# LoRA product from f16 halves with powers of two, in 512-column chunks and PSUM banks of its own, and another order of y's transposes

## The reference, cut to what matters

```python
x = x + tanh(g_xattn) * matmul(fake_quant(layernorm(x)), fake_quant(ctx))    # x: 2 x 1024 x 2048
y = layernorm(x)
logits = y @ gate_w.T + expert_bias                                          # 4 experts
one_hot = onehot(argmax(logits))
base = y @ W_up.T                                                            # 2048 x 2048
z = einsum('nh,erh->ner', y, lora_A)                                         # rank 8 for each expert
delta = einsum('neh,ne->nh', einsum('ner,ehr->neh', z, lora_B), one_hot)
x = x + tanh(g_ffn) * (base + delta)
```

## Time and profile before

| | us |
|---|---|
| median of 3 runs | 967.28 (966.79 to 969.95) |
| the profiled execution, its own time | 968.11 |
| its span, first to last instruction | 966.3 |
| TensorE busy | 938.9 |
| VectorE busy | 411.3 |
| ScalarE busy | 229.9 |
| products of stage 2 (line 980), 3840 matmuls | 686.7 |
| products of stage 1 (line 912), 1024 matmuls | 226.4 |
| `lora` (line 987), 80 matmuls | 29.1 |

### The profile page before, as it was taken

The page is one execution under the profiler, slowest core; times in us unless marked ns, Lnnn a source line. Parts: engine busy times, 40 slices in busy tenths (PEclk is TensorE's granted clock), DMA queues, the critical chain, the costliest instruction groups (busy, mean ns, idle before and its releaser), DMA issues.

```text
span 966.3 us, 12221 instructions
## 1 busy us (share of the span) xinstructions
PE 938.9 (97%) x5280; PEld 505.9 (52%) x5280; DVE 411.3 (43%) x829; ACT 229.9 (24%) x192; POOL 15.3 (2%) x39
## 2 busy tenths in 40 slices
PE   2899999999999999999999999999999999999998
PEld 0444444444455555555555555555555555555554
DVE  6694757785867404132332404232332404232301
ACT  5886777777540000000000000000000000000000
POOL 0001000000000000000000000000000000000000
PEclk9999999999999999999999999999999999999999
DMA  8999977678543233222322132222223222121211
GB/s 348 420 375 390 419 290 287 220 296 303 195 177 78 88 87 88 88 44 87 44 87 70 67 110 60 88 44 87 44 88 77 64 78 44 44 44 44 44 45 44
DMA packets 77018, 135.25 MB, mean 140 GB/s; under 512 B 61889, under 2 KB 62017, under 8 KB 62657
## 3 DMA queue, kind: packets, MB, share of 16 engines
q1 hardware_dynamic: 71200, 93.52, 29.7%
q0 software_dynamic: 3312, 24.12, 6.4%
q10 hardware_dynamic: 2448, 16.78, 4.2%
HBM read 90.36 MB, written 29.37 MB: 124 GB/s over the span
## 4 chain that ended last, share of the span: by engine, by line
PE 91%; DVE 4%; DMA 2%; ACT 1%; issue 1%; SPq 0%; DVEq 0%; ACTq 0%
PE bank L980 66%; PE bank L912 21%; PE bank L987 2%; PE bank L889 1%; DVE arena L660 1%; DMA stage<-in_b_t 1%; DMA rows<-in_x 1%; DVE bn L570 1%; DMA normed<-in_w 1%; ACT arena L396 1%; ACT arena L414 0%; DVE rows_T L680 0%; DVE rows L630 0%; DVE b_stack L721 0%; DVE halves L668 0%
## 5 line engine op out<-in xcount | busy, mean ns | idle before, releaser
L980 PE MATMUL bank<-arena,rows_T 128*128 128x416 f16 (+1 forms) x3840 | 686.7, 339 | 0.0
L980 PEld LDWEIGHTS bank<-arena,rows_T 128*128 128x128 f16 x3840 | 369.7, 97 | 302.8 <-issue 8.2
L912 PE MATMUL bank<-arena,rows_T 128*128 128x512 bf16 x1024 | 226.4, 382 | 3.2 <-ACT rows_T L388 2.3
L912 PEld LDWEIGHTS bank<-arena,rows_T 128*128 128x128 bf16 x1024 | 99.7, 98 | 122.2 <-issue 3.8
L728 DVE SCALAR_TENSOR_TENSOR rows<-bank,derived,rows 128x416 f32<-128x416 f32 (+2 forms) x80 | 48.4, 640 | 252.9 <-PE bank L987 252.9
L435 ACT ACTIVATE z_stack_T<-bank 96x128 fp32r<-96x128 f32 x16 | 4.4, 273 | 565.3 <-PE bank L994 565.3
L570 DVE BATCH_NORM_STATS2 bn<-rows 128x6 f32<-128x512 f32 x124 | 76.8, 680 | 6.0 <-DMA rows<-in_x 3.8
L630 DVE SCALAR_TENSOR_TENSOR rows<-bank,derived,rows 128x512 f32<-128x512 f32 x60 | 44.7, 747 | 23.8 <-PE bank L912 23.3
L694 DVE SCALAR_TENSOR_TENSOR route<-bank,derived,scal 128x4 f32<-128x4 f32 x16 | 3.5, 221 | 115.9 <-PE bank L980 115.8
L396 ACT ACTIVATE arena<-arena,scal,derived 128x2048 int16<-128x2048 f32 x22 | 45.0, 2084 | 2.8 <-DMA arena<-in_ctx 2.8
L670 DVE SCALAR_TENSOR_TENSOR halves<-normed,ln,halves 128x2048 f16<-128x2048 f32 x14 | 32.9, 2351 | 29.0 <-ACT halves L429 29.0
(11 more groups left out here) (89 smaller groups left out, 253.9 us busy)
## 6 DMA issues: line engine op xcount, KB each, us to landing
arena<-in_ctx SPq DMA_DIRECT2D x22, 1024.0 KB, 17.0
stage<-in_w SPq DMA_DIRECT2D x17, 1042.0 KB, 5.5
out<-rows ACTq DMA_DIRECT2D x15, 1024.0 KB, 3.9
h_scratch<-rows POOLq DMA_DIRECT2D x11, 1024.0 KB, 7.4
rows<-h_scratch SPq DMA_DIRECT2D x11, 1024.0 KB, 4.9
stage<-in_ctx SPq DMA_DIRECT2D x10, 1024.0 KB, 12.3
rows<-in_x POOLq DMA_DIRECT2D x10, 1024.0 KB, 9.4
normed<-in_w SPq DMA_DIRECT2D x7, 1042.0 KB, 6.3
```

Source lines behind the costliest of these rows:

```text
L912: mm = mmul(bk, q1T[:, t % 4, kt, :], Q(b, n, kt), start=(kt == 0), stop=(kt == KT - 1 and not slow), skip_group_check=True)
L980: mm = mmul(bank[c][:, 0:b - a], YT[:, s % 2, yh, kt, :], W(kt, wh, a, b), start=(first and kt == kts[0] and yh == 0 and wh == 0), stop=False,
```

## The change

- The stack of z and the B stack are f16 instead of f32 or fp32r. Ahead of that z (already multiplied with the scale of the product) is multiplied with a row of powers of two, one for each row of B, and divided by a power of two of its own token; B's rows are divided by theirs. `route` grows from 9 linked instructions to 14, and one more writes the factor that takes the scale back (`gl`).
- `lora` works in four chunks of 512 columns that go to banks 5 and 6 in turn, no more into the banks of the products. The last product of a chunk closes its group. Chunks 0 and 1 of `lora` stand behind chunk 2 of the products, chunks 2 and 3 behind chunk 3, and none behind chunk 4. For tile 0 they stand inside tile 1: chunks 0 and 1 behind its chunk 0, and 2 and 3 in the midst of its chunk 1.
- `epi2` waits for the products alone; a new `epi_delta` adds the LoRA part, four times for each tile. `store2` waits for both. On VectorE epi2(s, 0) stands ahead of the moments of the next tile.
- lora_B is loaded by POOL, ahead of the maximum over the partitions, into the row buffer 0. ScalarE sums its magnitudes after y_high(0), `b_scale` makes the powers in four small instructions after epi(15, 3), and POOL sends them through HBM to all partitions. ScalarE makes the high half after the last weight, and `b_low` makes the low one in place of `b_stack`. POOL's load of row tile 20 stands behind all that.
- Group (0, 2) of y's transposes goes to bank 7 and stands directly behind (0, 1). Tile 0 starts block by block as the groups come out. Groups (1, 2) and (1, 3) stand behind chunk 4 of tile 0, and their `yT_out` behind the `epi2` of tile 0. Tile 1 does blocks 0 to 7 of its chunks 0 and 1 ahead of the wait for the other groups.
- The f32 identity is gone.

```diff
...
-        with nc.sbuf_tensor("stage1", [P, WC], F32) as S1:
-            pass
-        Bst = sb("b_stack", [P, WC], F32R)[0:ZR, 0:D]
-        Braw = S1[0:ZR, 0:D]
+        S1 = sb("stage1", [P, WC], F32)
+        Bst = S1[:, :].bitcast(F16)[0:ZR, 0:D]
+        Braw = X[0:ZR, 0, :]
...
+        YB = [[TR[0], TR[1], bank[7][:, :], TR[0]], [TR[0], TR[1], TR[0], TR[1]]]
+        ZP = bank[7][:, :].bitcast(F16)[0:ZR, 0:P]
...
                 load_w(i)
-            sp.wait_ge(s_lo, 15)
-            sp.dma_start(Braw, b_t).then_inc(s_braw, 16)
             sp.wait_ge(s_wc, 1)
...
+            nc.gpsimd.dma_start(Braw, b_t).then_inc(s_braw, 16)
             pool.wait_ge(s_pm, 1)
             nc.gpsimd.partition_all_reduce(V["PM"], V["pm"], P, bass.bass_isa.ReduceOp.max).then_inc(s_PM, 1)
+            pool.wait_ge(s_bp, 2)
+            nc.gpsimd.dma_start(brow_d, bp[0:E * R, 1:2]).then_inc(s_br0, 16)
+            pool.wait_ge(s_br0, 16)
+            nc.gpsimd.dma_start(br[:, :], brow_d.rearrange("k o -> (k o)").unsqueeze(0).to_broadcast(
+                [P, E * R])).then_inc(s_br, 16)
+            pool.wait_ge(s_bst, 1)
+            row(TILES + KEEP)
         @block.scalar
...
                 act.wait_ge(s_zt, s + 1)
                 if s >= 1:
-                    act.wait_ge(s_dl, 5 * s)
-                A(zT[:, :].bitcast(F32R), ZP, ACT.Copy).then_inc(s_ze, 1)
+                    act.wait_ge(s_dl, NL * s)
+                A(zT[:, :], ZP, ACT.Copy).then_inc(s_ze, 1)
...
                 u = TILES + s
                 act.wait_ge(s_e2, 5 * (s + 1))
+                act.wait_ge(s_el, NL * (s + 1))
                 act.dma_start(o_t[rows_of(s)], Xt(u)).then_inc(s_st[slot(u)], 16)
...
+            act.wait_ge(s_braw, 16)
+            act.wait_ge(s_mm, place[(TILES - 2, NCH - 1)] + 1)
+            A(q1T[0:ZR, (TILES - 2) % 4].rearrange("p k m -> p (k m)"), Braw, ACT.Abs,
+              accum_out=bp[:, 0:1]).then_inc(s_bs, 1)
             sqrt(TILES + 1)
             for n in range(8, 14):
                 w_high(n)
             y_high(1)
             for n in range(14, KT):
                 w_high(n)
+            act.wait_ge(s_lo, KT)
+            act.wait_ge(s_bp, 4)
+            A(Bst, Braw, ACT.Identity, scale=bp[:, 2:3]).then_inc(s_bhi, 1)
             z_out(0)
...
-                                     rt[:, 2, :].unsqueeze(2).to_broadcast([P, E, R]), ALU.mult))
+                zs = z0[:, 0, :]
+                link(v.scalar_tensor_tensor(out=zs.rearrange("p (e r) -> p e r", e=E),
+                                            in0=Z.rearrange("p (e r) -> p e r", e=E), scalar=V["sc2"],
+                                            in1=rt[:, 2, :].unsqueeze(2).to_broadcast([P, E, R]),
+                                            op0=ALU.mult, op1=ALU.mult))
+                if s == 0:
+                    dve.wait_ge(s_br, 16)
+                link(v.tensor_tensor(z0[:, 1, :], zs, br[:, :], ALU.mult))
+                link(v.tensor_scalar(z0[:, 2, :].bitcast(I32), z0[:, 1, :].bitcast(I32), 0x7FFFFFFF, None,
+                                     ALU.bitwise_and))
+                link(v.tensor_reduce(zp[:, 0:1], z0[:, 2, :], AX.X, ALU.max))
+                link(v.tensor_scalar(zp[:, 1:2], zp[:, 0:1], 2.0 ** -100, 2.0 ** 126, ALU.max, ALU.min))
+                link(v.tensor_scalar(zp[:, 2:3].bitcast(I32), zp[:, 1:2].bitcast(I32), 0x7F800000, None,
+                                     ALU.bitwise_and))
+                link(v.reciprocal(zp[:, 3:4], zp[:, 2:3]))
+                link(v.tensor_scalar(z0[:, 3, :], z0[:, 1, :], zp[:, 3:4], ZS, ALU.mult, ALU.mult))
+                v.tensor_scalar(gl[:, s % 2:s % 2 + 1], zp[:, 2:3], V["tf"], 1.0 / (ZS * WS), ALU.mult,
+                                ALU.mult).then_inc(s_gl, 1)
                 if s >= 1:
                     dve.wait_ge(s_zt, s)
                 for i in (0, 2):
-                    link(v.tensor_scalar(zb[:, i, :].bitcast(I32), z0[:, :].bitcast(I32), HIGH, None,
-                                         ALU.bitwise_and))
-                link(v.tensor_tensor(zb[:, 1, :], z0[:, :], zb[:, 0, :], ALU.subtract))
+                    ins = v.tensor_copy(zb[:, i, :], z0[:, 3, :])
+                    if i == 0:
+                        link(ins)
+                    else:
+                        ins.then_inc(s_zs, 1)
+                v.tensor_tensor(zb[:, 1, :], z0[:, 3, :], zb[:, 0, :], ALU.subtract).then_inc(s_zs, 1)
                 assert k[0] == LINKS
-                dve.sem_inc(s_zs, 1)
-            def b_stack():
-                dve.wait_ge(s_braw, 16)
-                dve.wait_ge(s_yl, 2)
-                v.tensor_scalar(T[0:ZR, 0:D].bitcast(I32), Braw.bitcast(I32), HIGH, None,
-                                ALU.bitwise_and).then_inc(s_bhi, 1)
+            def b_scale():
+                dve.wait_ge(s_bs, 1)
+                v.tensor_scalar(bp[:, 0:1], bp[:, 0:1], 2.0 ** -100, 2.0 ** 126, ALU.max, ALU.min).then_inc(s_bp, 1)
+                dve.wait_ge(s_bp, 1)
+                v.tensor_scalar(bp[:, 1:2].bitcast(I32), bp[:, 0:1].bitcast(I32), 0x7F800000, None,
+                                ALU.bitwise_and).then_inc(s_bp, 1)
+                dve.wait_ge(s_bp, 2)
+                v.reciprocal(bp[:, 0:1], bp[:, 1:2]).then_inc(s_bp, 1)
+                dve.wait_ge(s_bp, 3)
+                v.tensor_scalar(bp[:, 2:3], bp[:, 0:1], WS, None, ALU.mult).then_inc(s_bp, 1)
+            def b_low():
                 dve.wait_ge(s_bhi, 1)
-                v.tensor_copy(Bst[0:64, :], T[0:64, 0:D]).then_inc(s_bst, 1)
-                v.tensor_tensor(Bst[64:ZR, :], Braw[64:ZR, :], T[64:ZR, 0:D],
-                                ALU.subtract).then_inc(s_bst, 1)
+                v.scalar_tensor_tensor(out=Bst[64:ZR, :], in0=Braw[64:ZR, :], scalar=bp[64:ZR, 2:3], in1=Bst[64:ZR, :],
+                                       op0=ALU.mult, op1=ALU.subtract).then_inc(s_bst, 1)
             def epi2(s, c):
...
                 a, b = max(CUT[c], EXT), CUT[c + 1]
-                dve.wait_ge(s_dl, 5 * s + c + 1)
+                dve.wait_ge(s_m2, 5 * s + c + 1)
+                if c == 4 and s > 0:
+                    dve.wait_ge(s_el, NL * (s + 1))
                 xs = Xc(s + TILES, a - EXT, b - EXT)
                 v.scalar_tensor_tensor(out=xs, in0=bank[c][:, a - CUT[c]:b - CUT[c]], scalar=V["gs"], in1=xs,
                                        op0=ALU.mult, op1=ALU.add).then_inc(s_e2, 1)
+            def epi_delta(s, j):
+                dve.wait_ge(s_dl, NL * s + j + 1)
+                dve.wait_ge(s_gl, s + 1)
+                dve.wait_ge(s_e2, 5 * s + (5 if s == 0 else (3, 3, 4, 4)[j]))
+                xs = Xc(s + TILES, j * NB, (j + 1) * NB)
+                v.scalar_tensor_tensor(out=xs, in0=TR[j % 2], scalar=gl[:, s % 2:s % 2 + 1], in1=xs,
+                                       op0=ALU.mult, op1=ALU.add).then_inc(s_el, 1)
             moments(0)
...
             yT_out(0, 3)
             epi(15, 3)
+            b_scale()
             for n in range(9, 14):
                 w_low(n)
             norm(1)
             w_low(14)
             w_low(15)
             y_low(1)
-            b_stack()
+            b_low()
             route(0)
-            for g in range(4):
-                yT_out(1, g)
+            yT_out(1, 0)
+            yT_out(1, 1)
             for c in range(5):
                 epi2(0, c)
+            yT_out(1, 2)
+            yT_out(1, 3)
             for s in range(1, TILES):
+                if s == 1:
+                    epi_delta(0, 0)
+                    epi_delta(0, 1)
                 route(s)
+                if s == 1:
+                    epi_delta(0, 2)
+                    epi_delta(0, 3)
+                epi2(s, 0)
                 if s + 1 < TILES:
                     moments(TILES + s + 1)
                     norm(s + 1)
                     y_low(s + 1)
-                for c in range(5):
-                    epi2(s, c)
+                epi2(s, 1)
+                epi2(s, 2)
+                epi_delta(s, 0)
+                epi_delta(s, 1)
+                epi2(s, 3)
+                epi_delta(s, 2)
+                epi_delta(s, 3)
+                epi2(s, 4)
         @block.tensor
...
                             y_transposes(0, 0)
                             y_transposes(0, 1)
+                            y_transposes(0, 2)
                         if n == 2 and t == TILES - 1:
-                            y_transposes(0, 2)
                             y_transposes(0, 3)
...
+                    pe.wait_ge(s_epi, NCH * (TILES - 1))
                 else:
-                    pe.wait_ge(s_ye, 4 * s + g - 1)
+                    pe.wait_ge(s_ye, {0: 1, 1: 4 + g - 1}[s])
                 for i in range(8):
                     h, k = i // 4, 4 * g + i % 4
...
-            def lora(c):
-                a, b = max(CUT[c], EXT), CUT[c + 1]
```

(100 more changed lines are left out.)

18 lines of the change are left out of this document (8 added, 10 removed).

## The result

The changed kernel takes 964.92 us (median of 20 runs, 963.7 to 967.78), the one before 968.17 in the same series (20 runs). The ratio, estimated over the series, is 0.9971, with a 95% interval of 0.9965 to 0.9977: 2.8 us faster (the two medians alone differ by 3.25), where I had forecast 6.1. I had started from 967.28 us, a median of 3 runs, so some 0.9 of the 3.7 us between 964.92 and my 961.2 is the starting point.

What follows compares the result with a forecast made beforehand. TensorE, busy 97% of the span, was taken as the bound. Gains of 1.8 us in settled tiles and 4.25 in the turn, 6.1 in all, took 967.28 to 961.2 us; range 959.0 to 965.0, own range 959.5 to 962.5.

Steps and rivals of the forecast that it cites:

- The pace: TensorE streams: each matmul costs its columns at 2.4 per ns and 2.5 ns more.
- part 1: Settled tiles 1 to 15: f16 `lora` and transpose gain 0.18 us a tile; 1.8 us after tile 0's `lora`.
- All that VectorE got more: Longer `route`, a small instruction and four `epi_delta`: fifteen links take 3.35 us, hidden by 4.9 us of slack.
- rival C: Settled tiles: the longer `route` holds TensorE at the transpose of z, 984 us at 0.65 a link; 4%.
- Part 2: The turn between stage 1 and stage 2: TensorE's standing and small work there shrink, 4.25 us gained.
- steps (a) to (c): Turn: y's group (0, 2) moved, 1.14 us; fewer transposes before tile 1, 1.97; tile 0's five `lora` moved out, 1.14.
- (a): Turn: with y's group (0, 2) in its own bank, chunk (15, 3) starts 1.14 us earlier.
- the cover in part 2: Turn: last `w_low` ends near 291.5, TensorE asks at 292.2; 0.6 us slack, nothing taken for later weights.
- rival B: Turn: weights late by a powers DMA, `b_scale` or ScalarE's sum, 1 to 2.3 us over slack, 962.2 to 963.5; 12%.
- rival A: Settled tiles: 96-row weight loads of `lora` show, up to 5.4 us less gained, up to 966.6; 10%.

Runs made afterwards that it cites:

- e8: Kernel before with only the stack of z and the B stack in f16, z's fixed factor not taken back: 965.24 us, ratio 0.9972.
- e4: Full kernel after, but POOL sends the powers of B only when 14 weights are ready: 962.31 us, ratio 0.9947.
- e1: Kernel after without both DMAs of B's powers, ones in place of the powers: 962.0 us, ratio 0.9943.
- e3: Kernel after without the store of the powers; the 16 KB load stays, from an input: 962.25 us, ratio 0.9948.
- e7: Kernel before plus a POOL store of 32 x 4 bytes to unused HBM behind stage 1's last epi: 971.3 us, ratio 1.0039.
- e10: Kernel before plus a POOL store of 32 x 4 bytes to SBUF instead of HBM: ratio 1.0003.
- e9: Kernel before plus a POOL store of 32 rows of 512 bytes to HBM: ratio 1.0004.
- e11: Kernel before plus a POOL store of 128 bytes from one partition to HBM, as one piece: median 968.23 us, ratio 1.0011.
- e2: Kernel after with the store of the powers kept and the load back left out, ones in its place: 965.13 us, ratio 0.9974.
- e6: Kernel after with the store of the powers issued by ScalarE's queue instead of POOL's: 963.6 us, ratio 0.996.

## Why the prediction was right and wrong

- **The pace** of columns and 2.5 ns, and with it part 1: right. 43.22 us a tile for 43.2, and e8 shows that f16 as such brings 2.7 us, not the 0.79 us a tile, some 12 us, that columns alone would give.
- **All that VectorE got more**: hidden, as said, so rival C did not happen. I had miscounted, though: `route` now has 17 instructions, not 15, since the second copy and the subtraction at its end are not among the 14 linked ones. They take 3.6 us (883.43 to 887.01) for 3.35, and the transpose of z comes at 891.67, 4.7 us after them; the next tile waits for nothing.
- **Part 2, steps (a) to (c)**: right in size. With the store out of the way the turn is 44.15 us for 44.1, and (a) alone is 1.14 in the rows and 1.2 in time. From the first batch of transposes to tile 1 the kernel before takes 57.25 us (254.25 to 311.50) and e4 53.01 (254.63 to 307.64): 4.24 for 4.25.
- **The step that failed** is the cover in part 2, in the words "The two DMAs of B's powers (128 bytes, and 16 KB) run beside weight loads", and the choice "between nothing and one weight instruction I take nothing". The store makes the last weight 3.3 us late (295.2 for the 291.9 of e4), where the slack was 0.6. That is rival B, named with that very DMA in it but with 12%; its sign came, a gap of TensorE (292.8 to 295.3) released by the last weight's low half. Its price of 1 to 2.3 us was too small twice: the stand is 2.7 us in the profiled execution, and the lower clock behind it, of which I had said nothing, adds 1.7 there and likely in some 8 of 20 runs. e1, e3 and e4 give back 2.6 to 2.9 us of the kernel after, and e7 takes away 3.8.
- **The range**: that 964.92 lies inside 959.0 to 965.0 is luck. It is above what I had given B (963.5), and the range reached so far for rival A, which did not happen.
- **What is left**: e4 gained 5.3 per mille, 5.1 us, where 6.1 had been worked out. Between the profiled executions (968.11 and 962.48) it is 5.6, and there the sum closes: 4.24 in the turn, 1.74 behind it for the 1.8 of part 1 (from the start of tile 1 to the end of the span, 654.80 us before and 653.06 in e4), less 0.38 by which e4's first batch of transposes starts later. That start varies without the change too: in kernels with the same code up to there the first product of stage 2 starts anywhere from 263.54 (e7, e8) over 264.24 to 264.73 (e10). So a few tenths up to a us of a single execution can't be put on a step.

A row that could have warned me stood in the profile of before, though not among my rows: the store of `wback`, 8 KB in 4-byte pieces, took 12.4 us to land (source, engine, count, KB, us to landing):

```profile
w_back_row<-wback SPq DMA_DIRECT2D x1, 8.0 KB, 12.4
```

The Trainium skill, "DMA: Bandwidth & Descriptors", section "Specifications", says that below 512 bytes the DMA engine does a read-modify-write. e7 (4 bytes) against e9 (512) agrees with such a bound; e10, 4-byte pieces too but within SBUF, lost nothing, and e11, one piece below the bound, does little. Why 32 such writes hold the reads of 16 engines for 3 us no run here shows.

## What to carry to other kernels

Count a store of many 4-byte pieces to HBM as an event that may hold the loads beside it for some us (3.3 here), not as its bytes, and put it where no load is on the path: here one line moved it and nearly doubled the gain. When a cover has 0.6 us of slack, price what lies behind it in full, the clock after a stand included. And take a stream's pace from long runs of the trace before calling the rest of a tile overhead: here it turned the 12 us of f16 into 3.

## What the runs showed of the hardware that I had not expected

- 32 writes of 4 bytes to HBM, issued by POOL about 2 us ahead of a 1 MB load, delayed the loads by some 3 us (weight 13 in 9.7 to 10.1 us instead of 6.4 to 6.6, in e2 and e7). The same bytes within SBUF (6.7 us), or 16 KB in pieces of 512 bytes (6.4), delayed next to nothing.
- Waits of TensorE amid full work were followed by some us at 1.2 GHz in some executions and not in others. It fell behind a stand of 2.53 us (kernel after) and of 2.31 (e2), and behind three waits of 0.5 to 1.1 us (e11); it stayed at 2.4 GHz behind stands of 2.04 (e7) and 1.52 (e6), and behind waits of 0.4 to 1.1 us in the earlier trace rows.
- Two `lora` with stationaries of 96 rows amid products of 128 rows cost just their pace, 0.43 us.
